# Cross-attention of a decoder: the weighted context is moved out of PSUM by ScalarE instead of VectorE and GpSimd

## What is computed

```python
def xattn(hidden_q, kv_c, Wq, w_kc_q, w_kc_kv, W_qr, W_kr, Wo):
    q_hk = (hidden_q @ Wq.T).reshape(b, s, H, K)
    q_big = einsum('bshk,hkq->bshq', q_hk, w_kc_q)   # with rotary positions in layers 0 and 2
    kv_rope = kv_c * cos + rotate_half(kv_c) * sin
    q_r = einsum('bshq,hqr->bhsr', q_big, W_qr)
    k_r = einsum('bld,hdr->bhlr', kv_rope, W_kr)
    scores = einsum('bhsr,bhlr->bhsl', q_r, k_r)
    attn = softmax(scores, axis=-1)
    ctx_c = einsum('bhsl,bld->bhsd', attn, kv_rope)  # the weighted context
    ctx_lat = einsum('bhsd,hkd->bshk', ctx_c, w_kc_kv)
    return ctx_lat.reshape(b, s, H * K) @ Wo.T
x = layernorm(x + xattn(x, ctx, ...))
```

## Time and profile before

| | |
|---|---|
| median of 3 runs | 1696.13 us (1692.6 to 1697.54) |
| the profiled execution's own time | 1697.4 us |
| its span, first to last instruction | 1695.6 us |
| mean granted TensorE clock | 0.985 |
| busy: TensorE, VectorE, ScalarE, GpSimd | 1639.0, 1112.7, 746.7, 246.9 us |
| share of the chain that ended last: TensorE, VectorE | 87%, 5% |

### The profile page before, as it was taken

The page is one execution under the profiler, slowest core; times in us unless marked ns, Lnnn a source line. Parts: engine busy times, 40 slices in busy tenths (PEclk is TensorE's granted clock), DMA queues, the critical chain, the costliest instruction groups (busy, mean ns, idle before and its releaser), DMA issues.

```text
span 1695.6 us, 35593 instructions
## 1 busy us (share of the span) xinstructions
PE 1639.0 (97%) x15222; PEld 1114.4 (66%) x15222; DVE 1112.7 (66%) x1961; ACT 746.7 (44%) x1282; POOL 246.9 (15%) x432
## 2 busy tenths in 40 slices
PE   8999999999999899999999999999999999999998
PEld 4586367777755666655367777764566757777765
DVE  2734789999566753256889999535454279999632
ACT  2223366666412542134366666312444266666411
POOL 0021200000010312011300000020465000000030
PEclk9999999999999999999999999999999899999999
DMA  5322010000040011051020000050300220000010
GB/s 204 102 67 81 1 76 2 2 2 2 2 184 1 2 58 40 1 117 61 1 95 2 2 3 2 2 238 1 63 1 1 112 88 2 2 2 2 2 44 11
DMA packets 35422, 71.10 MB, mean 42 GB/s; under 512 B 25259, under 2 KB 29675, under 8 KB 31333
## 3 DMA queue, kind: packets, MB, share of 16 engines
q1 hardware_dynamic: 35266, 68.83, 12.2%
HBM read 68.36 MB, written 0.46 MB: 41 GB/s over the span
## 4 chain that ended last, share of the span: by engine, by line
PE 87%; DVE 5%; DMA 3%; ACT 2%; issue 1%; POOL 1%; SPq 0%; ACTq 0%; DVEq 0%; POOLq 0%
PE ps L1077 14%; PE ps L1090 13%; PE ps L993 13%; PE ps L337 9%; PE ps L1444 9%; PE ps L904 3%; PE ps L2501 3%; DMA arena<-in_ctx_sin 3%; PE ps L1105 3%; PE ps L1885 2%; PE ps L914 1%; PE ps L484 1%; PE ps L2528 1%; PE ps L975 1%; PE ps L940 1%
## 5 line engine op out<-in xcount | busy, mean ns | idle before, releaser
L1186 ACT ACTIVATE arena<-ps,softmax_stats 128x1500 f32<-128x1500 f32 x168 | 254.0, 1512 | 196.7 <-DVE softmax_stats L1267 194.7
L1090 PEld LDWEIGHTS ps<-arena,ctx_pos 125*64 125x64 f32 x4608 | 222.3, 137 | 58.4 <-issue 57.6
L1077 PE MATMUL ps<-ident,arena 64*125 64x64 f32 x4032 | 240.8, 272 | 6.4 <-ACT arena L1186 6.4
L1077 PEld LDWEIGHTS ps<-ident,arena 64*125 64x125 f32 x4032 | 229.1, 187 | 21.7 <-issue 13.8
L1090 PE MATMUL ps<-arena,ctx_pos 125*64 125x128 f32 (+1 forms) x4608 | 240.5, 262 | 0.0
L993 PE MATMUL ps<-ctx_feat,arena 64*128 64x500 f32 x1008 | 234.6, 599 | 0.0
L1193 ACT COPY arena<-ps 125x512 f32<-125x512 f32 x336 | 172.5, 599 | 79.3 <-PE ps L1077 79.3
L1265 DVE TENSOR_REDUCE softmax_stats<-ps 128x1 f32<-128x500 f32 x252 | 170.7, 679 | 53.4 <-PE ps L993 53.4
L337 PE MATMUL ps<-arena 128*128 128x256 f32 x736 | 174.4, 383 | 3.5 <-ACT arena L2596 1.0
L1278 DVE TENSOR_SCALAR arena<-arena,softmax_stats 128x1500 f32<-128x1500 f32 x168 | 168.3, 1002 | 5.9
L1444 PE MATMUL ps<-x_feat,arena 128*128 128x448 f32 (+1 forms) x416 | 167.9, 549 | 1.2 <-DVE arena L1545 1.2
(11 more groups left out here) (310 smaller groups left out, 1941.6 us busy)
## 6 DMA issues: line engine op xcount, KB each, us to landing
ctx_pos<-in_ctx SPq DMA_DIRECT2D x1, 3000.0 KB
arena<-in_L1f_gate SPq DMA_DIRECT2D x1, 2304.0 KB, 12.4
arena<-in_L1f_up SPq DMA_DIRECT2D x1, 2304.0 KB, 17.4
arena<-in_L1f_down SPq DMA_DIRECT2D x1, 2304.0 KB, 7.8
arena<-in_L0a_Wq SPq DMA_DIRECT2D x1, 2048.0 KB, 10.4
arena<-in_L0a_Wc SPq DMA_DIRECT2D x1, 2048.0 KB, 11.0
arena<-in_L0x_Wq SPq DMA_DIRECT2D x1, 2048.0 KB, 10.0
arena<-in_L0x_Wo SPq DMA_DIRECT2D x1, 2048.0 KB, 8.1
```

Source lines behind the costliest of these rows:

```text
L1077: m = nc.tensor.transpose(c.ps[0:LP, turn_bank(i, k, r), n * 64:(n + 1) * 64], probs[i % 2][e][rows, l * LP:(l + 1) * LP], c.ident[rows, r ...
L1090: m = nc.tensor.matmul(y[r * 64:(r + 1) * 64, lo:hi], c.ctx_pos[:, j, l, e, :], pT[i % 2][:, lo // 64:hi // 64, LT * e + l, :], start=(l = ...
L1186: nc.scalar.activation(probs[i % 2][e].rearrange("p (k l) -> p k l", k=3), sc[e], ACT.Exp, bias=low[:, i % 4, e:e + 1], accum_out=total[:, ...
```

## The change

`keep(i - 2)` moves from VectorE to ScalarE, where it stands behind the two exps of step i and ahead of the copies of turned probabilities. It no longer copies to `held` but writes each part to its place in `ctxT`, as two or four copies that raise `ct_in`. VectorE's `keep`, GpSimd's copies, the tiles `held` and the semaphore `kept` are gone, with the waits for them. TensorE's wait ahead of the third group of transposes is now for the copies of the unit before. `keep_last` stays as it is.

```diff
@@ core: tiles and semaphores
-    held = [c.at(o["RB"] + 128 * i, 128) for i in range(2)]
-    maxed, turned_lo, turned_hi, d_in, a_in, pv_mm, kept, ct_in, ct_last = (
+    maxed, turned_lo, turned_hi, d_in, a_in, pv_mm, ct_in, ct_last = (
...
@@ GpSimd
         pool.wait_ge(padded.handle, padded.last())
-        for i in range(NU - 1):
-            j, u = i // UNITS, i % UNITS
-            pool.wait_ge(kept.handle, kept.at(i + 1))
-            for r, e, lo, hi in parts(u):
-                rows, at = slice(r * 64, (r + 1) * 64), 128 * u - HALF * (r ^ e)
-                nc.gpsimd.tensor_copy(ctxT[rows, 2 * j + e, at + lo:at + hi], held[i % 2][rows, lo:hi]).then_inc(*ct_in.next())
-        pool.wait_ge(ct_in.handle, ct_in.last())
@@ TensorE, turn(i, k)
             if k == 2 and i > 0:
-                pe.wait_ge(kept.handle, kept.at(i))
+                pe.wait_ge(ct_in.handle, ct_in.at(placed(i - 1)))
@@ ScalarE
+        def keep(i):
+            act.wait_ge(pv_mm.handle, pv_mm.at(i + 1))
+            j, u = i // UNITS, i % UNITS
+            for r, e, lo, hi in parts(u):
+                rows, at = slice(r * 64, (r + 1) * 64), 128 * u - HALF * (r ^ e)
+                nc.scalar.copy(ctxT[rows, 2 * j + e, at + lo:at + hi], c.ps[rows, 6, lo:hi]).then_inc(*ct_in.next())
+
         for i in range(NU + 1):
             if i < NU:
                 exp(i, 0)
                 exp(i, 1)
+            if i >= 2:
+                keep(i - 2)
@@ VectorE
-        def keep(i):
-            dve.wait_ge(pv_mm.handle, pv_mm.at(i + 1))
-            if i >= 2:
-                dve.wait_ge(ct_in.handle, ct_in.at(placed(i - 2)))
-            nc.vector.tensor_copy(held[i % 2], c.ps[:, 6, 0:128]).then_inc(*kept.next())
-
...
                 normalise(i, 0)
-            if i >= 2:
-                keep(i - 2)
             if i >= 1:
                 copy_turned(i - 1, 0)
```

More of the change, by code:

```diff
@@ L776, in cross_attention @@
         [s.sem(x + "_%d" % e) for e in range(2)] for x in ("scored", "lowered", "exped", "recip", "normed"))
-    maxed, turned_lo, turned_hi, d_in, a_in, pv_mm, kept, ct_in, ct_last = (
-        s.sem(x) for x in ("maxed", "turned_lo", "turned_hi", "d_in", "a_in", "pv_mm", "kept", "ct_in", "ct_last"))
+    maxed, turned_lo, turned_hi, d_in, a_in, pv_mm, ct_in, ct_last = (
+        s.sem(x) for x in ("maxed", "turned_lo", "turned_hi", "d_in", "a_in", "pv_mm", "ct_in", "ct_last"))
     cm_mm, padded = s.sem("cm_mm"), s.sem("padded")
```

## The result

The changed kernel takes 1715.92 us (median of 4 runs, 1711.46 to 1716.19) against 1694.37 for the kernel before (median of 4). The ratio is 1.0119, with a 95% interval of 1.0094 to 1.0144: 21.5 us slower. 1722 was forecast, with 1706 to 1738 as the range.

What follows compares the result with a forecast made beforehand. TensorE, busy 97%, was taken as the bound; 66 stalls of 0.30 and 12 of 0.47 us add 25.4 to 1697.4 (1722.8) or the median 1696.1 (1721.5), said as 1722; range 1706 to 1738.

Steps and rivals of the forecast that it cites:

- Bound and place: Loop: TensorE, busy 97% of the span, sets the 8.1 us step; only a wait put into its order counts.
- Items 1 and 2: Loop: VectorE losing 81 copies (23 us busy) and GpSimd losing 186 copies are each worth 0.
- Item 3: ScalarE behind both exps: copies of 0.26 or 0.21 us, 0.02 apart, starting 0.03 behind the accumulator read; pair ends 304.15.
- Item 4: TensorE's wait before the third group of transposes: release 0.05 after the copies, start 304.20 for 303.90, 0.30 us stall a step.
- Items 5 and 6: Straddling unit: four copies, 0.47 us stall; count over three stages: 66 x 0.30 + 12 x 0.47 = 25.4 us.
- Item 7: ScalarE's later copies of turned probabilities: first starts 304.17 instead of 304.11, cost 0 with over 1 us to spare.
- A: ScalarE's copies fit by overlapping the accumulator read and each other: TensorE loses 0.02 a step, 1697, not slower; chance 0.10.
- B: TensorE's clock falls from the new stalls: 10 us more (1732) or 88 more (1810); chance 0.05.
- C: ScalarE's copies are dear, each near 0.34 us, or release takes longer: up to 42 us, 1738; chance 0.10.
- D: ScalarE's copies overlap among themselves as 128-row copies do: lower bound, 12 us, 1708; chance 0.15.

Runs made afterwards that it cites:

- the control with that wait moved: Kernel before, third group of transposes taken as 8 of rows 64 to 127, the wait, 8 of rows 0 to 63: 1733.73 us, loop 224.89.
- the last experiment: Changed kernel with VectorE's maximum for e = 1 taken over the first 500 of the 1500 scores: 1704.28 us, loop 215.95.

## Why the prediction was right, and where terms were off

**Bound and place (right).** TensorE sets the step, and only the wait ahead of the third group matters: the control with that wait moved leaves nothing of the change in the loop.

**Items 1 and 2 (right in effect).** VectorE's and GpSimd's copies were worth 0. VectorE's busy time fell only to 1102.5, not to 1090: the removed copies had overlapped their neighbours.

**Item 3, the copies (durations right, start wrong for most steps).** 64x128 takes 0.257 on average over its own form (0.26 was forecast), 64x64 takes 0.204 (0.21); a pair takes 0.53 to 0.54 (0.54), four in turn 0.89 (0.90). One mis-sized term is "The first can start 0.03 behind the accumulator read, as the second exp does". That holds for 30 steps, where rows 64 to 127 come first. In the other 48 the copies start 0.10 before the read ends. The row it came from had two causes ending together, ScalarE's read at 301.95 and VectorE's maximum, and the prediction read the wrong one; the last experiment separates them. That 0.03 fits the 30 steps is luck: there the turn to other rows makes it.

**Item 4 (release right, due time too late).** Release to start was 0.05 in all 78 steps, as forecast. The other mis-sized term is the time at which the third group is due. The prediction divided 2.69, from the start of the first load to the end of the last, by 48, and so had 32 x 0.056 = 1.79 and 303.90. The loads overlap, and the group starts 1.74 behind the first, at 303.85. Every wait is 0.05 longer than the sum had it. So u > 3 pays 0.34 where 0.30 was forecast, with copies that end when they were forecast to end. For u < 3 the copies are done 0.14 sooner than forecast: 0.20 against 0.30. In the straddling step they are done 0.13 sooner: 0.38 against 0.47.

**Items 5 and 6.** The count of 66 and 12 was right, but 66 falls into 36 and 30. The sum is 22.0 us in place of 25.4. The two errors have opposite signs: the late start of the copies is worth 36 x 0.13 + 12 x 0.12 = 6.1 us too much, the late due time 78 x 0.05 = 3.9 us too little, and the rest, 1.2 us, is 0.015 a step. The mechanism was right; that the sum came out as near as it did is in part luck.

**Item 7 (right).** No wait for the later copies lengthened a step: with the copies in place but the third group's wait moved, the loop was equal to its control.

**Rivals.** A: the first half of its mechanism is real (the overlap with the read), the second isn't for two halves of the rows, and both would have been needed. B: the loop's clock stayed up, at a granted clock of 1.00, the 2.4 GHz level, with 1.96 us of TensorE idle over a whole loop. This is the one of layer 0 in the changed kernel, and the other two show 1.00 as well (us, busy of PE, PEld, DVE, ACT, POOL; granted clock, DMA, GB/s):

```profile
231.07:450.54 219.47, 217.51 (x3021) 167.52 (x3021) 189.62 (x284) 151.69 (x268) 0.00 (x0) 1.00 0.01 2
```

C didn't come. D, the overlap among the copies, came only where the same rows follow each other. The rule that stood beside it, of the Trainium skill (ScalarE: Activation LUTs, What ACT_TABLE_LOAD costs: neighbours overlap by about 93 ns), fits the overlap with the accumulator read (0.10) for copies of all rows and of rows 0 to 63, and the overlap of two copies of the same rows (0.10). It doesn't fit copies that turn to other rows; there the measurement decides, and it is a gap of 0.02. Its 0.293 for a copy of 128 columns was above the 0.257 measured.

## What to carry to other kernels

Before work is moved to an engine to take a hop out, look at who waits for its result and when: a copy that ends 0.5 us early on one engine may end 0.15 to 0.3 us late on another, and on the bounding engine's order every step then pays. When a start time is read from a row, list all that ended just before it; two causes that end together can't be told apart by that row. When instructions overlap, the start of the 33rd is neither 32/48 of a merged row nor the end of the first 32: narrow the window until it has a row of its own. Where an output must be written in parts by rows, order the parts so that the same rows follow each other.

## What the runs showed of the hardware that wasn't expected

- ScalarE starts a copy 0.10 us before the accumulator read ahead of it ends if the copy takes all rows or rows 0 to 63, and 0.02 to 0.03 after its end if it takes rows 64 to 127.
- Copies of half the rows overlap by 0.10 us when the rows stay the same and leave a gap of 0.02 when they change: four of 64x64 take 0.64 us with one change of rows and 0.89 with three. The same instructions, in another order. The rows written may count as well: the four of 64x224 of the earlier trace rows read the same rows in pairs but write to changing ones, and none of them overlaps (4 x 0.340 + 3 x 0.02 = 1.42, for a measured 1.43). No run tests that by itself, and why a change of rows leaves a gap stays open.
- 16 transposes of 64 rows cost 0.49 us more when 8 of the same rows follow each other than when the halves take turns.
- Behind a wait of 0.21 to 0.39 us in the middle of a row of transposes, the 16 behind it load in 0.95 us, as without a wait: nothing was paid for the restart.
